# Seven late value tiles on six slots, keys ahead of attention, a reordered drain, and operands on one base remainder, in an fp32 transformer block on one core

## The reference, cut to what matters

```python
def reference(x, itok, cond_w, wq, wk, wv, wo, cond2_w, qweight, w_scale, bias):
    # x: 32 batches x 32 channels x 512; one 32x32 matrix of 16 for each batch
    h = einsum('bct,bcd->bdt', x, cond_w[itok])
    q, k, v = h @ wq, h @ wk, h @ wv       # 32 heads, 8 key/value heads, 128 wide
    q, k = rope(q), rope(k)
    s = q @ k.T / sqrt(128)                # per batch and head 32 x 32, causal mask
    o = softmax(s) @ v
    x = x + o @ wo                         # wo: 4096 x 512
    y = einsum('bct,bcd->bdt', x, cond2_w[itok])
    a = fp8_quantized(y)                   # scale: largest |y| / 448
    f = a @ fp8(qweight).T * w_scale + bias
    return x + clip(f / f_scale) * f_scale
```

## Time and profile before

| | |
|---|---|
| median of three runs | 550.5 us (546.47 to 550.77) |
| profiled execution, its own time | 551.23 us |
| its span | 549.4 us |
| mean granted clock of TensorE | 0.972 |
| TensorE busy | 515.3 us (94%), weight loads 407.5 us (74%) |
| VectorE, GpSimd, ScalarE busy | 422.1 us, 312.6 us, 251.2 us |

### The profile page before, as it was taken

The page is one execution under the profiler, slowest core; times in us unless marked ns, Lnnn a source line. Parts: engine busy times, 40 slices in busy tenths (PEclk is TensorE's granted clock), DMA queues, the critical chain, the costliest instruction groups (busy, mean ns, idle before and its releaser), DMA issues.

```text
span 549.4 us, 9239 instructions
## 1 busy us (share of the span) xinstructions
PE 515.3 (94%) x3150; PEld 407.5 (74%) x3150; DVE 422.1 (77%) x660; ACT 251.2 (46%) x477; POOL 312.6 (57%) x310
## 2 busy tenths in 40 slices
PE   8997999849999999999999999999999999799990
PEld 6886888638787878787888888887878787578530
DVE  5454667696787978797879788887978788765797
ACT  2434256256264636463555446354636453123424
POOL 1247668869838774875688568847884654000002
PEclk9999899978999999999999999999999999989996
DMA  8317311302042022104010401041200023000004
GB/s 262 122 39 245 118 40 38 116 0 58 10 146 57 1 80 75 57 0 153 0 57 0 153 0 57 0 153 34 89 30 20 1 82 116 0 2 1 0 0 153
DMA packets 32644, 35.27 MB, mean 64 GB/s; under 512 B 2251, under 2 KB 22859, under 8 KB 32620
## 3 DMA queue, kind: packets, MB, share of 16 engines
q1 hardware_dynamic: 32620, 34.96, 19.7%
HBM read 28.66 MB, written 6.29 MB: 64 GB/s over the span
## 4 chain that ended last, share of the span: by engine, by line
PE 88%; DVE 5%; POOL 2%; issue 2%; DMA 2%; ACT 1%; SPq 0%; DVEq 0%; ACTq 0%
PE bank L721 24%; PE bank L723 23%; PE bank L722 23%; PE bank L786 3%; PE bank L775 3%; DMA values<-v_st 2%; PE bank L693 2%; PE bank L695 1%; PE bank L694 1%; PE bank L664 1%; PE bank L844 1%; PE bank L921 1%; POOL o_lo L392 1%; PE bank L652 1%; PE bank L901 1%
## 5 line engine op out<-in xcount | busy, mean ns | idle before, releaser
L385 POOL TENSOR_TENSOR q_rot<-q_rot,q_swap 128x512 f32<-128x512 f32 x64 | 88.2, 1378 | 57.9 <-DVE q_swap L1046 57.9
L721 PE MATMUL bank<-wo_hi,o_hi 128*128 128x512 f32 x256 | 103.8, 405 | 3.5 <-issue 3.5
L722 PE MATMUL bank<-wo_lo,o_hi 128*128 128x512 f32 x256 | 102.1, 399 | 0.0
L723 PE MATMUL bank<-wo_hi,o_lo 128*128 128x512 f32 x256 | 102.0, 398 | 0.0
L513 ACT ACTIVATE q_swap<-bank 64x512 f32<-64x512 f32 x80 | 47.6, 596 | 81.7 <-PE bank L723 35.5
L1094 DVE TENSOR_TENSOR xacc<-xacc,bank 128x512 f32<-128x512 f32 x64 | 43.8, 684 | 42.8 <-PE bank L723 42.3
L530 ACT ACTIVATE o_hi<-bank 128x512 fp32r<-128x512 f32 x64 | 33.0, 604 | 73.2 <-PE bank L786 73.2
L721 PEld LDWEIGHTS bank<-wo_hi,o_hi 128*128 128x128 f32 x256 | 48.7, 190 | 17.2 <-issue 5.5
L1046 DVE TENSOR_TENSOR q_swap<-q_swap,cst 128x512 f32<-128x512 f32 x80 | 61.4, 767 | 0.0
L723 PEld LDWEIGHTS bank<-wo_hi,o_lo 128*128 128x128 f32 x256 | 48.8, 191 | 11.9
L722 PEld LDWEIGHTS bank<-wo_lo,o_hi 128*128 128x128 f32 x256 | 48.8, 191 | 10.8
(11 more groups left out here) (161 smaller groups left out, 1094.0 us busy)
## 6 DMA issues: line engine op xcount, KB each, us to landing
raw_q<-in_L_attn_wq SPq DMA_DIRECT2D x16, 512.0 KB, 4.1
raw_o<-in_L_attn_wo SPq DMA_DIRECT2D x8, 1024.0 KB, 7.2
v_st<-values SPq DMA_DIRECT2D x16, 256.0 KB, 4.4
xacc<-in_x SPq DMA_DIRECT2D x4, 512.0 KB, 7.5
raw_k<-in_L_attn_wk SPq DMA_DIRECT2D x8, 256.0 KB, 4.4
values<-v_st SPq DMA_DIRECT2D x8, 256.0 KB, 2.0
out<-xacc SPq DMA_DIRECT2D x8, 256.0 KB, 2.0
raw_o<-in_L_attn_wv SPq DMA_DIRECT2D x1, 1024.0 KB, 8.1
```

Source lines behind the costliest of these rows:

```text
L385: pool.tensor_tensor(item_out(h, k), item_out(h, k), q_swap[(h + k) % 2][:], ALU.add).then_inc(rope_done, 1)
L721: pe.matmul(dst, l_hi, r_hi, start=(i == 0), stop=False)
L722: pe.matmul(dst, l_hi, r_lo, start=False, stop=False)
L723: mm = pe.matmul(dst, l_lo, r_hi, start=False, stop=(i == n - 1))
```

## The change

- **Values.** V_LATE becomes 7 and V_SLOTS 6. `V_BEFORE = (9, 11, 14, 16)` says how many value tiles are made before the end of what stands ahead of each of the first halves: nine ahead of half (0,0), then two in it, three in (0,1) and two in (1,0). The slots are s_exp, p_tr, two new tiles v_more, and the two v_st. VectorE's order in the opening is written out by hand; in a half the first late copy stands ahead of the last rotary item, the others where they all stood.
- **SP.** Stores 0 to 4 ahead of the wait for wv's low parts, wq of half (0,0), stores 5 and 6, wq of (0,1), stores 7 and 8, then wo.
- **Keys ahead of attention.** On TensorE `key` stands ahead of `attend`, and waits for the first rotary product of the half before instead of for all five. On ScalarE the swap of item 0 stands ahead of the four o_hi, on VectorE rope 0 ahead of the four o_lo.
- **Opening on ScalarE.** The four t_hi stand ahead of the seven wq_hi.
- **Drain.** On VectorE `round_w8(0)` moves one accumulation up, and the four o_lo of unit (7,0) move ahead of the last accumulation of unit (6,1).
- **End.** VectorE adds all eight tiles itself, in the order clip(t), add(t-1). BY_POOL with ScalarE's scaling and GpSimd's adds is gone.
- **Addresses.** s_max, s_sum and s_rec (64 bytes a partition each) move from between o_lo and w_sum to the front. All that is allocated between (hT, t, q_rot, o_hi, o_lo, o2, wo7 and the rest up to o_lo) lies 192 bytes higher; w_sum and all behind it (wq, wk, wo) stay or move by 4096. Base addresses modulo 512 bytes, before: hT, t, o, o2, wo7 64, but wq, wk, wo 256 (the single slices of them lie multiples of 512 further). After: all 256.

```diff
-V_LATE = 4
-V_SLOTS = 4
-BY_POOL = (1, 3)
+V_LATE = 7
+V_SLOTS = 6
+V_BEFORE = (9, 11, 14, 16)
...
+        s_max, s_sum, s_rec = (sb(n, [P, TPU * REP]) for n in ("s_max", "s_sum", "s_rec"))
...
+                v_more = [sb(f"v_more{i}", [P, 512], F32, steady) for i in range(2)]
...
-            for i in range(4):
+            for i in range(5):
                 store_values(i)
             sp.wait_ge(wv_lo_done, 2 * KC)
             load_pair(0, 0)
+            store_values(5)
+            store_values(6)
             load_pair(0, 1)
+            for i in range(7, V_BEFORE[0]):
+                store_values(i)
             sp.dma_start(raw_o[:], wo_v[:, 0:REP, :]).then_inc(dma_o, 16)
-            for i in range(4, 2 * TILES - V_LATE):
-                store_values(i)
...
             def half(g, h, last=None, fill=()):
 
                 n = 2 * g + h
+                key(g, h)
                 if last is not None:
                     pe.wait_ge(rope_cos, 5 * n)
-                    if h == 0:
-                        pe.wait_ge(s_turned, 2 * g)
                     attend(*last)
-                key(g, h)
                 pair(g, h, last)
...
-                    pe.wait_ge(rope_cos, 5 * (2 * g + h))
+                    pe.wait_ge(rope_cos, 5 * (2 * g + h) - 4)
...
             accumulate(KV - 2, 1, 1)
+            round_w8(0)
             accumulate(KV - 2, 1, 2)
-            round_w8(0)
-            accumulate(KV - 2, 1, 3)
             for b in range(BPT):
                 o_low(KV - 1, 0, b, o2_ps)
+            accumulate(KV - 2, 1, 3)
...
             clip(0)
-            clip(1)
-            add_back(0)
-            clip(2)
-            clip(3)
-            add_back(2)
-            clip(4)
-            add_back(4)
-            clip(5)
-            clip(6)
-            add_back(5)
-            clip(7)
-            add_back(6)
-            add_back(7)
+            for t in range(1, TILES):
+                clip(t)
+                add_back(t - 1)
+            add_back(TILES - 1)
```

More of the change, by code:

```diff
@@ L254, in unit_of @@
             return (g - 2, 1) if h == 0 else (g - 1, 0)
-        late = range(2 * TILES - V_LATE, 2 * TILES)
+        late = [range(V_BEFORE[n], V_BEFORE[n + 1]) for n in range(3)]
         block = ctx.enter_context(nc.Block())
@@ L532, in _ @@
             k_high(0)
+            for i in range(4):
+                t_high(i)
             for i in range(PRODUCTS):
                 q_high(0, 0, i)
-                if i < 4:
-                    t_high(i)
             def half(g, h, last=None, soft=None, split_wo=None):
@@ L713, in _ @@
             mix(7)
-            for i in range(TPU, 2 * TILES - V_LATE):
+            for i in range(TPU, V_BEFORE[0]):
                 values(i)
@@ L740, in pair @@
                 product(g, h, 0)
+                if isinstance(g, int) and n < 3:
+                    pe.wait_ge(t_lo_done, 4)
+                    if n > 0:
+                        pe.wait_ge(rope_cos, 5 * n)
                 product(g, h, 1)
@@ L826, in half @@
                     project_out(*last, 3)
-            half(0, 0, fill=late[0:2])
-            half(0, 1, fill=late[2:4])
-            half(1, 0)
+            half(0, 0, fill=late[0])
+            half(0, 1, fill=late[1])
+            half(1, 0, fill=late[2])
             half(1, 1, last=(0, 0))
@@ L1007, in _ @@
             h_low(7)
-            for i in range(TPU, 2 * TILES - V_LATE):
-                v_copy(i)
-                if i < 2 * TPU:
-                    t_sum(i - TPU)
-                else:
-                    t_low(i - 2 * TPU)
+            t_sum(0)
+            t_sum(1)
+            v_copy(4)
+            t_sum(2)
+            t_sum(3)
+            v_copy(5)
+            t_low(0)
+            v_copy(6)
+            t_low(1)
+            t_low(2)
+            v_copy(7)
+            t_low(3)
+            v_copy(8)
             def block_sum(g, h, step):
@@ L1107, in half @@
                 soft_part(0, 1, 2)
+                rope(g, h, 0)
                 if last is not None:
@@ L1138, in _ @@
             dve.wait_ge(dma_const, 32)
-            half(0, 0, fill=late[0:2])
-            half(0, 1, fill=late[2:4])
-            half(1, 0, weights=(0, 0))
+            half(0, 0, fill=late[0])
+            half(0, 1, fill=late[1])
+            half(1, 0, weights=(0, 0), fill=late[2])
             half(1, 1, last=(0, 0), weights=(0, 1))
```

50 lines of the change are left out of this document (21 added, 29 removed).

## The result

The changed kernel takes 532.76 us (median, 532.47 to 537.23) against 550.42 us before (546.47 to 550.77). The ratio of the means, 533.8 and 549.5, is 0.971, with a 95% interval of 0.967 to 0.975; that of the medians is 0.968. By the medians 17.7 us were won where 25.5 were forecast (525, range 519 to 533), by the means 15.7: the direction is right, the amount is not. The median sits at the upper edge of the range, the mean outside it. The profiled executions differ by 18.7 us in span (549.4 and 530.7), and the rest of this text splits those.

What follows compares the result with a forecast made beforehand. TensorE was taken as the bound, with 88% of the chain. Opening 2.7, first four halves 11.1, keys 0, remainder 6.0, drain 5.9 and end 0.6 sum to 26.3 us off 551.23: 525 us, range 519 to 533.

Steps and rivals of the forecast that it cites:

- item (d): Half (1,1): VectorE comes late out of the softmax, then has rope 0 and o_lo; a loss of 0.6 us.
- Opening: Opening: value-slot wait (3.3 us) and clock loss (1.6) go, new copy waits cost 2.2; net gain 2.7 us.
- The rival with a halved clock there: Opening: the new copy waits grow to 3.3 us and the clock halves for a time, giving 528; chance 0.06.
- Half (0,1): Half (0,1): the third value tile covers the wait for the last rotary add, gaining 1.8 us.
- (1,0): Half (1,0): two tiles and the key cover the probabilities wait (7.3 us), and the half clock goes (2.6 us).
- Keys ahead of attention, price 0: Loop: same matmuls; o_lo ends 2.3 us after attention, two products cover 2.7 us, so price 0.
- one remainder, 6.0: Products, keys and projections: equal base remainders modulo 512 give all the 226.4 ns pitch, gaining 6.0 us.
- the remainder does nothing: Rival on matmul pitch: equal base addresses modulo 512 bring no gain, giving 531; chance 0.18.
- each base by itself: Rival on matmul pitch: each operand's base counts alone, all pairs get 235.7 ns, giving 539.5; chance 0.07.
- Drain: Drain: o_lo ahead of the last accumulation wins 2.9 us of wait and 3.0 of half clock; 5.9 us.
- 1.00 from the opening to 500 us: Profile after: the granted clock would stay at 1.00 from the opening to 500 us.
- The slower side: Halves with attention: key ahead uncovers o_lo; up to 532, chance 0.05, or slower, 557, chance 0.02.

Runs made afterwards that it cites:

- Experiment 2: Changed kernel with ScalarE's wo_hi made at the end of half (0,1), three of GpSimd's four wo_lo in (1,0), the fourth at the start of (1,1): 528.11 us.
- 3: Changed kernel with one value tile moved from half (0,1) to half (1,0): 534.12 us.
- 4: Changed kernel with keys behind attention again on TensorE, ScalarE and VectorE: 535.78 us.
- 9: Kernel of Experiment 2 with, in half (0,0), GpSimd's rotary add 1 and ScalarE's swap 1 moved earlier: 526.89 us.
- 10: Changed kernel with VectorE's t_lo writing only 8 of 512 columns, TensorE multiplying t_hi in their place: 528.95 us in one run.
- 7: Changed kernel with VectorE's old order in the opening, each value copy ahead of each t_full sum, t_lo behind all copies: 532.79 us.
- 11: Changed kernel with s_max, s_sum and s_rec allocated where they were, so the old base remainders return: 538.52 us.
- 1: Kernel before with only s_max, s_sum and s_rec allocated ahead of hT, giving equal base remainders: 544.56 us against 549.84.
- 8: Changed kernel with 128 bytes of padding ahead of each of wq_hi, wk_hi and wo_hi: 540.55 us in one run.
- 5: Changed kernel with VectorE's old drain order, last accumulation of unit (6,1) and first weight rounding ahead of the four o_lo: 536.92 us.
- 6: Changed kernel with GpSimd again adding two of the eight last tiles at the end: 532.37 us.
- 12: Changed kernel with 256 bytes of padding ahead of wq_hi, so wq, wk and wo stand 256 bytes from hT, t and o: 532.76 us in one run.

## Why the prediction was off, step by step

- **The first four halves, item (d): the step that failed.** "In half (1,1) VectorE comes late out of the softmax ...: I charge 0.6 us." The half lost 5.6. The mechanism was another one: the sentence looked at VectorE's list and never at GpSimd's. The rows were at hand: the stretch 103.9 to 127.5 of the earlier trace rows has GpSimd busy for 16.95 us, and with the 7.3 us wait gone and two tiles of work put in, the stretch became 18.9 us long; GpSimd's next list then holds 5.2 us of wo_lo more than the half before it. In place of VectorE's 0.6 us the runs showed GpSimd's last wo_lo ending at 126.38, 1.9 us after TensorE could have used it, a second stop of 2.1 us through GpSimd's rotary add, and 1.4 us of half clock. Experiment 2 took three wo_lo out of the half, put the fourth at its start, and got 5.4 us back; 3 and 4 gave GpSimd time in other ways and the stops shrank.
- **Half (0,0), not mentioned in the sum: 1.1 us.** The forecast wrote of VectorE's sums in the opening that they "overlap GpSimd's o_lo" and priced only VectorE's side, 2.2 us of copies. GpSimd's side was the larger thing: it leaves the opening 4.6 us behind the first product where before it was 6.0 ahead. Experiments 9 and 10.
- **Opening: 2.4 for 2.7.** Right in the sum, in part by luck. 0.7 of the 2.4 lie ahead of the first value matmul (18.69 before, 17.99 after), where kernels alike up to there spread from 17.98 to 19.05. The two waits were 1.9 and 1.6 (forecast 1.0 and 1.2), but 7 shows that they cost nothing beyond what GpSimd's chain takes anyway. The rival with a halved clock there didn't occur in the kernel after; it did in 7, behind a wait of 3.34 us.
- **Half (0,1): 1.3 for 1.8, and (1,0): 10.1 for 9.9.** The third tile covers the rotary add, no wait stands at attention, and the clock stays at 1.00. "By a hair" was apt: the probabilities are ready at 113.28, and TensorE's attention starts at 113.69.
- **Keys ahead of attention, price 0, and one remainder, 6.0.** Both right in size and wrong as separate terms. By 11 the remainder is worth 5.4 us in the new order (the whole kernel: 538.52 without it, 532.76 with it) and the key's place nothing by itself; by 1 and 4 the remainder without the key loses 2.6 us of it again. The forecast had the reason in a half sentence (the rotary chain moves 0.5 us earlier, "about as much as the faster pitch takes from it") and the square bears it out: 0.5 us a pass. Had the key stayed, 6.0 would have been 3.4 (an estimate: 6.0 less the 2.6). Of the rivals, "the remainder does nothing" is refuted by 1 and 11, where it alone changes, and "each base by itself" (235.7 ns everywhere) by 226.6 ns of 256 over 256. The Trainium skill (SBUF — State Buffer, Who interferes with whom) has TensorE's two read ports independent; by that alone, how the two bases stand to each other should not matter, and experiments 1, 8 and 11 go against it here. Why the bases matter no run shows.
- **Drain 5.8 for 5.9, end 0.7 for 0.6.** Right, by the mechanisms named (5 and 6), though by 5 the drain's clock part, half of its 5.8, may come in some executions only. VectorE's o_lo start at 474.02 in the last unit and 461.20 in the one before, and the stop that was 3.22 us is 0.35.
- **Clock.** The three stretches at 0.50 went as forecast, but "1.00 from the opening to 500 us" failed: the new stops of (1,1) brought one of 3.4 us, worth 1.4.
- **The slower side** (o_lo uncovered by the key ahead of attention): never near. TensorE has no wait for o_lo in the loop. The forecast counted 14 halves with attention; there are 13, from (1,1) to (7,1).

The sum with the terms as measured: 2.4 - 1.1 + 1.3 + 10.1 - 5.6 + 4.2 + 0.8 + 5.8 + 0.7 = 18.6 us of 18.7. The chances were too narrow in one way: all rivals put the trouble on TensorE's operands, on VectorE (with GpSimd only as what slows it), or on the loop, and none on the list of the engine that the removed wait had been sheltering.

## What to carry to other kernels

When a long wait of the bounding engine is filled with work, list for every other engine when it finishes each thing that the bounding engine needs in the next stage, and how long before the need; subtract from that lead what was filled. Here the last wo_lo was 2.9 us early before and 1.9 us late after. The start of a list alone doesn't tell: in 2 GpSimd starts its sums 3.5 us behind the half's first product, later than in the kernel after, and TensorE doesn't stop, since the wo_lo are made by then. Moving such work to a stage where its engine idles cost nothing here (5.4 us won, and 526.9 us for the whole kernel with 9). Follow a wait back through every engine that works in order: the one named may be the third in the row. And terms that shorten one engine's work and terms that clear the chain next to it don't add; price them together, or forecast each corner of the square.

## What the runs showed of the hardware

- **Matmul pitch and base addresses.** With 128x512 fp32r matmuls in the three-pass strings, the pitch is 226.6 to 227 ns where moving operand and weights stand on the same remainder modulo 256 bytes (256 over 256, 64 over 64, and in 12 256 over 0 and 0 over 256), and 1 to 3% more where they don't: 233.3 for projections and about 229 for products at 192 bytes apart, 233.4 and 230 to 232 at 128 apart. Other distances weren't tried. It showed as 5 us out of 530, for three small tiles allocated in another place.
- **VectorE beside GpSimd.** GpSimd's sum of 128x256 takes 0.74 us alone and 1.66 to 1.73 beside VectorE's t_lo (10). The Trainium skill (SBUF — State Buffer, Who interferes with whom) says that a VectorE instruction with two SBUF inputs contends with a GpSimd instruction that reads SBUF; this trace agrees, and both of t_lo's inputs lie in SBUF.
- **The clock after short stops.** Half (1,1) has the same first stop of 2 us in the kernel after, in 6, 7 and 11, but the stretch at 0.50 came behind the second stop in the first (at 135.4, 1.4 us lost), ahead of it in 6 (at 128.0, nothing lost), and not at all in 7 and 11: the half takes 32.5 us in the kernel after, 31.1 in the other three. A single profile's stretch of this kind is worth up to 1.5 us either way. What decides it stays open.
